# Expert slots by indirect DMA in place of dense experts, and a wfc bias taken into the matmul

## The reference, cut to what matters

```python
    x = x + jnp.tanh(g_xattn[0]) * _L0_xattn_ref(_layernorm(x), ctx_1024, ...)
    x = x + jnp.tanh(g_ffn[0]) * _L0_ffn_ref(_layernorm(x), L0_ffn_Wr, L0_ffn_We)
# attention: q, k with rms_norm for each head, softmax, then
        return x @ Wfc + fc_b
# experts: C = 97
        top_vals, top_idx = jax.lax.top_k(logits, K)
        w = jax.nn.softmax(top_vals, axis=-1)
        pos_all = jnp.cumsum(oh, axis=1) - oh
        keep = pos < C
        buf = jnp.zeros((Bb * Ee * C, Dd)).at[dst].add(x_rep, mode='drop')
        expert_out = jnp.einsum('becd,edf->becf', expert_in, We)
        gathered = jnp.take(expert_out, dst, axis=0, mode='fill', fill_value=0.0)
        out = jnp.einsum('btk,btkd->btd', w, gathered)
```

## Time and profile before

| what | value |
|---|---|
| time, median of 3 runs | 1391.57 us (1390.58 to 1393.33) |
| span of the profiled execution | 1388.5 us |
| TensorE busy | 1364.6 us, 98% |
| VectorE busy | 1046.5 us, 75% |
| ScalarE busy | 913.9 us, 66% |
| GpSimd busy | 775.2 us, 56% |
| granted TensorE clock, mean | 0.996 of full speed |
| data moved by DMA | 53.72 MB, mean 39 GB/s |

### The profile page before, as it was taken

The page is one execution under the profiler, slowest core; times in us unless marked ns, Lnnn a source line. Parts: engine busy times, 40 slices in busy tenths (PEclk is TensorE's granted clock), DMA queues, the critical chain, the costliest instruction groups (busy, mean ns, idle before and its releaser), DMA issues. The chain is left out here.

```text
span 1388.5 us, 26883 instructions
## 1 busy us (share of the span) xinstructions
PE 1364.6 (98%) x8116; PEld 1137.0 (82%) x8116; DVE 1046.5 (75%) x3057; ACT 913.9 (66%) x2600; POOL 775.2 (56%) x947
## 2 busy tenths in 40 slices
PE   7899999999999999999999999999999999999998
PEld 6688888888888888888888888888888888888876
DVE  6877877777877777877778777778777788777763
ACT  6776666775666766667766667666677666676652
POOL 4355555656555656555555566565555555555644
PEclk9999999999999999999999999999999999999999
DMA  5001101011111011110111010111110110101000
GB/s 164 30 18 46 45 28 45 18 45 45 37 37 45 18 46 45 32 42 25 38 45 45 29 45 18 45 45 36 38 39 24 45 45 31 43 18 46 25 16 23
DMA packets 70289, 53.72 MB, mean 39 GB/s; under 512 B 45888, under 2 KB 53504, under 8 KB 70144
## 3 DMA queue, kind: packets, MB, share of 16 engines
q1 hardware_dynamic: 70144, 52.00, 12.1%
HBM read 25.11 MB, written 16.78 MB: 30 GB/s over the span
## 5 line engine op out<-in xcount | busy, mean ns | idle before, releaser
L332 PE MATMUL bkM<-we,x2T 128*128 128x512 f32 x3072 | 791.7, 400 | 0.8 <-DVE acc_v L1067 0.7
L332 PEld LDWEIGHTS bkM<-we,x2T 128*128 128x128 f32 x3072 | 553.6, 188 | 127.6 <-ACT a_out L684 8.4
L684 ACT ACTIVATE a_out<-bkM,gate 128x256 f32<-128x256 f32 x512 | 217.0, 482 | 161.1 <-PE bkM L332 159.9
L1067 DVE SCALAR_TENSOR_TENSOR acc_v<-bkM,gate,acc_v 128x256 f32<-128x256 f32 x384 | 184.8, 481 | 106.2 <-PE bkM L332 91.3
L498 POOL TENSOR_TENSOR a_sum<-a_sum,a_out 128x256 f32<-128x256 f32 x256 | 188.9, 738 | 56.8 <-ACT a_out L684 20.5
L485 POOL TENSOR_TENSOR probs<-probs,p_inv 128x308 f32<-128x308 f32 x128 | 89.8, 702 | 211.6 <-DVE p_inv L960 211.6
L453 POOL TENSOR_TENSOR rstd<-ve,minus_half 128x4 f32<-128x4 f32 x64 | 65.2, 1019 | 145.6 <-DVE ve L872 145.4
L453 POOL TENSOR_TENSOR q_r<-q_ve,minus_half 128x8 f32<-128x8 f32 x64 | 105.0, 1642 | 48.6 <-DVE q_ve L945 48.6
L590 ACT ACTIVATE xn<-x_sb,shift,rstd 128x256 f32<-128x256 f32 x128 | 66.5, 590 | 92.4 <-DVE shift L881 92.4
L453 POOL TENSOR_TENSOR k_r<-k_ve,minus_half 77x8 f32<-77x8 f32 x32 | 52.4, 1637 | 126.9 <-DVE k_ve L921 126.9
L503 POOL TENSOR_TENSOR y<-a_sum,acc_v 128x256 f32<-128x256 f32 x128 | 94.4, 738 | 17.3 <-issue 0.4
(11 more groups left out here) (178 smaller groups left out, 2714.7 us busy)
## 6 DMA issues: line engine op xcount, KB each, us to landing
x_sb<-in_x SPq DMA_DIRECT2D x32, 512.0 KB, 3.7
out<-y SPq DMA_DIRECT2D x64, 256.0 KB, 2.0
ctx_sb<-in_ctx SPq DMA_DIRECT2D x32, 154.0 KB
vf<-v_nat SPq DMA_DIRECT2D x64, 77.0 KB
stage<-in_L_ffn_We SPq DMA_DIRECT2D x2, 1024.0 KB, 7.1
vf<-v_nat SPq DMA_DIRECT2D x32, 52.0 KB
vf<-v_nat SPq DMA_DIRECT2D x32, 51.0 KB
vf<-v_nat SPq DMA_DIRECT2D x32, 26.0 KB
```

The lines of the kernel that those rows point to most:

```text
L332: mm = nc.tensor.matmul(out, l, r, start=(i == 0), stop=(i == len(terms) - 1))
L684: ins = nc.scalar.activation(a_out[:, t % 2, (e // 4) * 2 + i], bkM[1][:, i * D:(i + 1) * D], ACT.Copy, scale=gate[:, m.parity, t, e:e + 1])
L1067: nc.vector.scalar_tensor_tensor(out=acc_v[:, t], in0=bkM[0][:, i * D:(i + 1) * D], scalar=gate[:, m.parity, t, e:e + 1], in1=src, op0=ALU ...
```

## The change

**Experts.** Instead of all experts for all tokens, the tokens' rows are sorted into expert slots through DRAM. `place` computes for each token and each of its two choices a row number. GpSimd scatters the rows of xn2 with indirect DMAs of 128 rows each, 4 for each batch, 8 for each pair. SyncE loads the slots back as 112 partitions of 8 rows (`load_rows`). Then eight units for each pair follow, of two experts of one batch: TensorE transposes 97 rows by 2 experts (4 transposes into the one bank bkM), ScalarE writes the hi part, VectorE the lo part, TensorE multiplies (12 matmuls of 256 columns into the one bank bkN), ScalarE copies out. SyncE stores the outcome (`store_rows`, two for each batch), GpSimd gathers with 8 indirect DMAs for each pair, and VectorE weights and adds both rows of each token (`combine`). Rows above the capacity of an expert stay zero in the outcome. The tables `T_AT` and `E_AT` say in which slot a unit is transposed and multiplied; units 6 and 7 and the product of unit 5 fall in the next round, where the pair is called c. The pipeline has one round more. x1 has three buffers, xn2 two.

**Bias.** fc starts each tile with two matmuls of a row of ones by the gated bias (hi, lo), and the residual reads the loaded x. GpSimd's four xb additions go.

Core of the diff:

```diff
+ROWS = 2 * LQ * (E // 2) * TOPK
+PAD = 112
+UNITS = BP * E // 2
...
+        slots_in = stage
+        slots_out = sb("slots_out", [P, 2, E // 2 * D])
+        slots_T = sb("slots_T", [P, 2, 2, KC * 2 * CAP], F32R)
+        fetched = sb("fetched", [P, TOPK, T, D])
...
+        in_d = [nc.dram_tensor(f"in_rows{b}", (ROWS, D), F32, kind="Internal").ap() for b in range(BP)]
+        out_d = [nc.dram_tensor(f"out_rows{b}", (ROWS, D), F32, kind="Internal").ap() for b in range(BP)]
...
-        front_banks_in_fill = [bkM[0], bkM[1]]
+        front_banks_in_fill = [bkM, bkN]
         kv_bank = [bkD, bkE]
...
+        T_AT = {7: (0, 0), 8: (0, 1), 9: (0, 2), 10: (0, 3), 11: (0, 4), 12: (0, 5), 2: (1, 6), 3: (1, 7)}
+        E_AT = {8: (0, 0), 9: (0, 1), 10: (0, 2), 11: (0, 3), 12: (0, 4), 1: (1, 5), 3: (1, 6), 4: (1, 7)}
+        def unit_at(table, k, c, m):
+            late, u = table.get(k, (0, None))
+            pair = (m, c)[late]
+            return (pair, u) if u is not None and pair else None
...
-            for n in range(PAIRS):
-                step(pair(n), pair(n + 1), pair(n + 2), pair(n + 3))
+            for n in range(PAIRS + 1):
...
+            def load_rows(m, b):
+                sp.wait_ge(stage_used, STAGE_USED)
+                sp.sem_inc(waits_alone, 1)
+                sp.wait_ge(scattered[b].sem, scattered[b].at(m))
+                sp.sem_inc(waits_alone, 1)
+                sp.wait_ge(unit_ps.sem, max(unit_ps.at(m, (b + 1) * UNITS_OF - UNITS), 0))
+                sp.sem_inc(waits_alone, 1)
+                sp.dma_start(slots_in[0:PAD, b], in_d[b][0:PAD * E].rearrange("(p j) d -> p (j d)", j=E)
+                             ).then_inc(rows_in[b].sem, 16)
+            def store_rows(m, b, i):
+                sp.wait_ge(expert_out.sem, expert_out.at(m, b * UNITS_OF + (i + 1) * UNITS_OF // 2))
+                sp.sem_inc(waits_alone, 1)
+                sp.wait_ge(gathered[b].sem, gathered[b].before(m))
+                sp.sem_inc(waits_alone, 1)
+                half = E // 2 * D
+                sp.dma_start(out_d[b][0:PAD * E].rearrange("(p j) d -> p (j d)", j=E)[:, i * half:(i + 1) * half],
+                             slots_out[0:PAD, i]).then_inc(rows_out[b][i].sem, 16)
...
+            def step(c, m, p, f, ahead):
+                if m:
+                    load_rows(m, 0)
+                if c:
+                    store(c, 0)
+                    store_rows(c, 1, 0)
+                if f:
+                    put_v(f)
+                if m:
+                    load_rows(m, 1)
+                if c:
+                    store_rows(c, 1, 1)
                 if ahead:
                     load(ahead)
-                if f:
-                    put_v(f)
-                store(m, 0)
-                store(m, 1)
+                if c:
+                    store(c, 1)
+                if m:
...
+            def scatter(m, b):
+                pool.wait_ge(cleared, CLEARS)
+                pool.sem_inc(waits_alone, 1)
+                pool.wait_ge(place_chain.sem, place_chain.at(m))
+                pool.sem_inc(waits_alone, 1)
+                pool.wait_ge(rows_in[b].sem, rows_in[b].before(m))
+                pool.sem_inc(waits_alone, 1)
+                for t in range(b * SUB, (b + 1) * SUB):
+                    for k in range(TOPK):
+                        nc.gpsimd.indirect_dma_start(
+                            out=in_d[b], out_offset=bass.IndirectOffsetOnAxis(ap=idx[:, m.parity, k, t:t + 1], axis=0),
+                            in_=xn2[:, m.parity, t], in_offset=None).then_inc(scattered[b].sem, 16)
+            def gather(m, b):
+                for i in range(2):
+                    pool.wait_ge(rows_out[b][i].sem, rows_out[b][i].at(m))
+                    pool.sem_inc(waits_alone, 1)
+                for t in range(b * SUB, (b + 1) * SUB):
+                    pool.wait_ge(y_done[t].sem, y_done[t].before(m))
+                    pool.sem_inc(waits_alone, 1)
+                    for k in range(TOPK):
+                        nc.gpsimd.indirect_dma_start(
+                            out=fetched[:, k, t], out_offset=None, in_=out_d[b],
+                            in_offset=bass.IndirectOffsetOnAxis(ap=idx[:, m.parity, k, t:t + 1], axis=0)
+                        ).then_inc(gathered[b].sem, 16)
+            def round_of(c, m, p, f):
                 if f:
                     ln1(f)
                 if m:
-                    finish_tile(m, 0)
+                    scatter(m, 0)
                 if p:
                     ln2(p)
+                if m:
+                    scatter(m, 1)
                 if f:
                     k_rsqrt(f)
-                if m:
-                    finish_tile(m, 1)
-                if f:
-                    make_xb(f, 0)
...
-                    make_xb(f, 3)
-                    make_xb(f, 2)
-                    normalise(f, 0)
-                    normalise(f, 1)
...
+            def unit_hi_part(m, u):
+                act.wait_ge(unit_ps.sem, unit_ps.at(m, u + 1))
+                act.wait_ge(expert_ps.sem, max(expert_ps.at(m, u - 1), 0))
+                copy(slots_T[:, u % 2, 0], bkM[:, 0:KC * 2 * CAP]).then_inc(unit_hi.sem, 1)
+            def expert_part(m, u):
+                b, i = divmod(u, UNITS_OF)
+                act.wait_ge(expert_ps.sem, expert_ps.at(m, u + 1))
+                h = i // 2
+                act.wait_ge(rows_out[1 - b][h].sem, rows_out[1 - b][h].at(m) if b else rows_out[1 - b][h].before(m))
+                act.wait_ge(cleared, CLEARS)
+                copy(slots_out[0:CAP, h, i % 2 * 2 * D:(i % 2 + 1) * 2 * D], bkN[0:CAP]).then_inc(expert_out.sem, 1)
...
+            def slot(k, c, m, p, f, xn_made=False):
+                next_unit(k, c, m)
                 if k == 0 and p:
                     o_part(p, 1)
...
                     if f:
                         exps(f, 0)
-                    chunk(k, m, p)
+                    unit_out(k, c, m)
                     if f:
...
                     if f:
                         o_part(f, 0)
+                if k != 9:
+                    unit_out(k, c, m)
 
...
             def residual(p, i):
                 dve.wait_ge(fc_ps.sem, fc_ps.at(p, i + 1))
-                dve.wait_ge(xb_done.sem, xb_done.at(p))
+                dve.wait_ge(x_in[p.parity], 16 * p.half + 16)
                 if i == 0:
                     dve.wait_ge(xn2_done.sem, xn2_done.before(p))
-                dve.wait_ge(v_added.sem, v_added.before(p, 2))
+                for t in range(T):
+                    dve.wait_ge(y_done[t].sem, y_done[t].before(p, X1_BUFS))
                 ts = slice(2 * i, 2 * i + 2)
-                nc.vector.tensor_tensor(x1[:, p.parity, ts], fc_bank[i][:].rearrange("p (t d) -> p t d", d=D),
-                                        xb[:, ts], ALU.add).then_inc(x1_done.sem, 1)
+                nc.vector.tensor_tensor(x1[:, p.n % X1_BUFS, ts], fc_bank[i][:].rearrange("p (t d) -> p t d", d=D),
+                                        x_sb[:, p.parity, ts], ALU.add).then_inc(x1_done.sem, 1)
                 dve.wait_ge(x1_done.sem, x1_done.at(p, i + 1))
...
+            def place(p):
                 dve.wait_ge(pos_done.sem, pos_done.at(p))
-                dve.wait_ge(v_added.sem, v_added.before(p, 2))
-                dve.wait_ge(a_ready.sem, a_ready.before(p, 2))
+                dve.wait_ge(top2.sem, top2.at(p))
+                nc.vector.tensor_tensor(placed[:], mask[:].rearrange("p k t e -> p k (t e)"),
+                                        pos_ps.unsqueeze(1).to_broadcast([P, TOPK, T * E]), ALU.mult
+                                        ).then_inc(place_chain.sem, 1)
+                dve.wait_ge(place_chain.sem, place_chain.at(p, 1))
+                nc.vector.tensor_reduce(row[:], placed[:].rearrange("p k (t e) -> p (k t) e", e=E), AX.X, ALU.add
+                                        ).then_inc(place_chain.sem, 1)
                 for b in range(BP):
-                    nc.vector.scalar_tensor_tensor(
-                        out=gate[:, p.parity, b * SUB:(b + 1) * SUB],
-                        in0=pos_ps.rearrange("p (s b e) -> p b s e", s=SUB, b=BP)[:, b], scalar=float(CAP),
-                        in1=g_all[:, b * SUB:(b + 1) * SUB], op0=ALU.is_lt, op1=ALU.mult
-                    ).then_inc(gate_chain.sem, 1)
...
+            def unit_lo_part(m, u):
+                dve.wait_ge(unit_hi.sem, unit_hi.at(m, u + 1))
+                lo(slots_T[:, u % 2, 1], bkM[:, 0:KC * 2 * CAP], slots_T[:, u % 2, 0]).then_inc(unit_lo.sem, 1)
...
+            def combine(c, b):
+                w = w_top[:, c.parity]
+                dve.wait_ge(gathered[b].sem, gathered[b].at(c))
+                dve.wait_ge(y_out[b].sem, y_out[b].before(c))
+                for t in range(b * SUB, (b + 1) * SUB):
+                    nc.vector.scalar_tensor_tensor(out=y[:, t], in0=fetched[:, 0, t], scalar=w[:, 0, t:t + 1],
```

(58 more changed lines are left out.)

309 lines of the change are left out of this document (126 added, 183 removed).

## The result

| | before | after |
|---|---|---|
| time, median | 1391.07 us (1389.38 to 1393.33) | 1679.91 us (1679.37 to 1687.64) |
| span of the profiled execution | 1388.5 us | 1677.9 us |
| granted TensorE clock, mean | 0.996 | 0.935 |
| data moved by DMA | 53.72 MB, 39 GB/s | 246.90 MB, 147 GB/s |

The changed kernel is slower by a ratio of 1.209 (95% interval 1.206 to 1.212). The forecast was 1495 us with a range of 1290 to 1590: the direction was right, the size was not, and the time lies outside the range.

What follows compares the result with a forecast made beforehand. TensorE's own stream sets today's 42.2 us round; after the change in-order waits make it 45.0. 1388.5 + 30 x 2.8 + 19 = 1491.5 of span, with 3.1 more 1495 us; range 1290 to 1590.

Steps and rivals of the forecast that it cites:

- the walk: One steady round followed in order from R, when TensorE is free after the last attend product; next R at 45.0.
- the ends: Fill unchanged in sum; after the last attend three rounds in series, 74 us instead of 55.5, +19.
- what bounds it: After the change, in-order waits between engines' streams; by work alone the round could close in 35 us.
- the clock: TensorE's clock counted at its full level, 1.00, despite idle pieces of 1 to 2 us.
- 8 bias matmuls of 256 columns at 1.41/12, 0.9: In fc on TensorE: the added bias matmuls cost 0.9 us a round.
- X: Time one indirect DMA of 128 rows holds GpSimd: taken as 1.1 us, with 0.87 and 1.64 kept.
- the middle: Exponentials: added hi parts, copies and waits put exps(3) at 36.6; with the combine's wait for gathers, 37.6.
- C: Rival: GpSimd becomes the bound; with X = 2 the round takes 50 us, the time 1645; chance 0.12.
- A: Rival: the round closes faster than the walk says, as streams' phases settle otherwise; 40.5 us, 1360; chance 0.23.
- B: Rival: TensorE's work alone decides; round of 37 us, 1255; chance 0.10.
- The load's landing: SyncE's load of 896 KB of rows takes 6.2 us, ahead of the store and gathers the combine waits for.
- Gap's 0.5 us: VectorE's gap priced at 0.2 us; 0.5 stays wherever normalise runs beside it, at most 1 us a round.

Runs made afterwards that it cites:

- combo: Changed kernel with 128-row ones and bias, unit 6 transposed ahead of fc, k_r ahead of the second scatters, rows' store ahead of load in SyncE's queue: 1537.20 us.
- bias_alone_rows: Kernel before with only the bias moved into fc, no xb additions, ones and bias operands of 128 rows: 1421.35 us.
- k_first: Changed kernel with GpSimd's k_r ahead of the second half's four scatters and a store of rows ahead of the load in SyncE's queue: 1640.07 us.
- combo_late_store: combo with VectorE's combine moved from slot 10 to the end of slot 12, and SyncE's output store put behind two stores of expert rows: 1492.42 us.
- units_only_xb: Changed kernel without scatters, gathers, row loads and stores, combining constant rows; unit 6 transposed ahead of fc, bias added on GpSimd: 1377.48 us.
- bias_alone: Kernel before with only the bias part of the change: one-row bias matmuls in fc, no xb additions, residual reads x: 1470.03 us.
- early6: Changed kernel with unit 6 transposed at step 1, ahead of the fc product instead of behind it: 1638.03 us.
- combo_store: combo with SyncE's output store put behind two stores of expert rows, the combine still in slot 10: 24 us slower than combo.

## Why the prediction was right in sign and wrong in size

Positions from R in the round at 865.59, against the walk:

| step | walk | measured |
|---|---|---|
| fc ends | 5.45 | 7.04 |
| unit 6's low part ends | 7.0 | 8.66 |
| shift | 8.7 | 10.3 |
| x_transpose | 10.9 | 12.6 |
| q | 14.6 | 17.0 |
| k_transpose | 18.7 | 21.8 |
| exps(0) | 27.5 | 31.3 |
| exps(3) | 37.6 | 41.6 |
| next R | 45.0 | 49.4 |

Two steps of the prediction failed: the round's sum, 45.0 where the settled rounds take 50.0, in the terms below, and the ends, +19 where they took +59. The waits themselves were right.

- **Right: what bounds it.** The waits that the walk named are in the trace at their places: VectorE idle 4.36 us ahead of unit 6's low part, x_transpose waiting for xn1, k_transpose for kn and kn for k_r, the second row maximum (0.67 us), unit 4's transposes behind unit 3's low part (1.49), the combine for its gathers (0.89). Three edits on them (unit 6's place; k_r's together with SyncE's order; the combine's on top of combo) gave back 1.3, 1.0 and 1.1 us a round by the traces.
- **The missing 5.0 us, in the walk's order.** Up to x_transpose 1.7, of which the bias is 1.6; from there to k_transpose 1.4; to exps(3) 0.9; to the next R 0.4. That is the round of the table, the only one wholly at the full clock. The other 0.6 go with the clock, as below.
- **Mis-sized: the bias.** The step "8 bias matmuls of 256 columns at 1.41/12, 0.9" was priced by full-height matmuls. The columns are right (bias_alone_rows: 0.98 a round), but the one-row operand costs 1.5 more. As it stands at the very front of the chain, the first four rows of the table are late by it and by little else. It is 49 us in the kernel before and 45 in the changed one, a quarter of what the forecast missed.
- **Mis-sized: X.** Taken as 1.1, measured 1.27. The four scatters between layernorm 2's power and k_r take 5.1 us instead of 4.4. That, a power of 1.2 us, and its start at 13.0 instead of 10.7 (1.6 of this is the bias) put k_transpose at 21.8. That the price matters from about there was right: k_r waited for scatters (k_ve ready at 883.27, k_r started at 884.91), and in k_first k_transpose is 1.4 us earlier; the round became 1.0 shorter.
- **Mis-sized: the middle.** From k_transpose to the fourth exps 19.8 us pass instead of 18.9; the combine's wait (1.1 us a round by combo against combo_late_store) was in the walk. What the walk did not say is that this wait takes back what is won ahead of it.
- **The clock.** The prediction counted it at its full level and said that no row showed otherwise. In the changed kernel 1 of the 28 settled rounds is wholly at that level, 49.4 us; 18 have a mean of 0.97 and take 49.5; 9 are at 0.93 or 0.90 and take 51.0. That is 0.6 us a round in the mean, some 17 us. That the lower level lengthens a round, and is not only its companion, is shown in combo_late_store alone.
- **The rivals.** C (GpSimd as the bound at X = 2, 1645) is the nearest number but not the cause: GpSimd is busy for 49% of the span, X is 1.27, and changing the order alone removes the delay. A's round of 40.5 isn't there: even units_only_xb, with no rows moved at all, has 41.8. B fails on order as the walk said; TensorE's own work in the round came to 38.3 us of busy time where 34.4 of work were summed. The bias is 1.6 of the difference (2.5 instead of 0.9); the rest is not divided, and busy time also counts a last matmul's way to PSUM at each piece of idle time.
- **The load's landing.** Estimated at 6.2 us by the rows' slope, measured 5.6, with the store behind it at 4.2. The fit of the Trainium skill ("DMA: Bandwidth & Descriptors", Anatomy of one DMA), 4.1 us, is further off; the page gives it for DMAs that GpSimd issues, and this load is SyncE's.
- **Wrong: the ends.** The step "router, place, scatters, load, units, store, gathers: 74, that is +19" gave +59. It put the last pair's place at 29 us and let the scatters follow it. VectorE's half of the router stands behind `combine`, which waits 7.29 us for gathered rows, and the place ends at 1605.09, 41.3 us after the last R at 1563.80:

```profile
1598.49 0.88 DVE L1127 SCALAR_TENSOR_TENSOR y<-fetched,w_top,x 128x256 f32<-128x256 f32 x2 [7.29 <-DMA fetched<-out_rows,idx]
...
1604.92 0.17 DVE L1108 SCALAR_TENSOR_TENSOR idx<-row,first 128x8 uint32<-128x8 f32 x1
```

  Then the scatters follow the gathers of the pair ahead in GpSimd's queue, 6.3 us more:

```profile
1606.38 0.95 POOL L563 DMA_INDIRECT fetched<-out_rows,idx  x1 [9.71 <-DMA out_rows<-slots_out]
...
1611.41 1.00 POOL L550 DMA_INDIRECT in_rows<-xn,idx  x1 [0.30 <-issue]
```

  so the first stands 47.6 us after that R, where the walk's router ended at 28. From there to the end 66.5 us pass instead of some 46. TensorE stands still for 6 to 7 us, for loaded rows or for a low part that is queued behind a combine, and then has the lower of its two clock levels (12 matmuls in 2.86 us instead of 1.64); over these last 114 us its granted clock is 0.70 in the mean:

```profile
1643.21 0.91 PE L1300 MATMUL bkM<-ident,stage 97*128 97x97 f32 x4 [6.03 <-DVE slots_T L919]
1643.82 2.86 PE L356 MATMUL bkN<-we,slots_T 128*97 128x256 f32 x12
```

- **The range.** It left room for X = 1.64 alone and none for several terms off the same way. 4.8 us a round over 30 rounds, of which about 1.5 is the bias, and 40 us of ends make the 185 missed.
- **Gap's 0.5 us.** It went, and what gap waits for can be read off the traces: a normalise on GpSimd. Before and after (VectorE's gap, then GpSimd's normalise, one round each):

```profile
732.21 0.69 DVE L1004 TENSOR_TENSOR gap<-top 128x4 f32<-128x4 f32 x1
```

```profile
732.18 0.70 POOL L485 TENSOR_TENSOR probs<-probs,p_inv 128x308 f32<-128x308 f32 x1 [1.85 <-DVE p_inv L960]
```

```profile
906.24 0.22 DVE L1063 TENSOR_TENSOR gap<-top 128x4 f32<-128x4 f32 x1
```

```profile
905.75 0.70 POOL L537 TENSOR_TENSOR probs<-probs,p_inv 128x308 f32<-128x308 f32 x1 [3.55 <-DVE p_inv L1019]
```

  Wherever the two overlap, in 31 of 32 gaps before and in 30 of 32 after, gap ends 0.02 us behind the normalise; without one beside it gap takes 0.16 us. In all but the first of them gap began 0.03 us behind the normalise's start before, and took its whole length; now it begins 0.5 us behind, and 0.2 us are left of it. That agrees with the rule of the Trainium skill ("SBUF — State Buffer", Who interferes with whom): gap has two SBUF inputs, and the normalise reads SBUF. Its 0.5 us went because the phase of the two shifted, and not by anything in the price of 0.2: that part of the sum came out by luck.

## What to carry to other kernels

In a pipeline of in-order streams, price a change by walking one round, and sum each term at the form it really has: a matmul operand of one row, or a DMA that GpSimd issues, has no near neighbour in the old trace and deserves a bound of its own at every place where it stands on the chain. When a step moves on one engine, move with it everything that waits for it in other queues, or the store behind it will hold up work that has nothing to do with it. Where two chains meet, as attention and the gathered rows do in the combine, shortening one gives back only what the other leaves. And walk the last rounds by the loop's own order, not by what the data would allow.

## What the hardware showed that was not expected

- A pair of 256-column float32r matmuls with one contraction row took 0.42 us, with 128 rows 0.24 us, and the six full ones behind it 0.91 instead of 0.71. The weight loads of the pair, in bias_alone and in bias_alone_rows, took the same:

```profile
340.33 0.29 PEld L1243 LDWEIGHTS bkA<-bias_r,ones_r 1*128 1x128 f32 x2
```

```profile
330.82 0.31 PEld L1243 LDWEIGHTS bkA<-bias_r,ones_r 128*128 128x128 f32 x2
```

  That agrees with the Trainium skill ("TensorE: Matmul & The Clock Gate", LDWEIGHTS), by which a load goes by its columns and not by its rows. So the loads are not longer. The single records of bias_alone show that they are later: where one row and 128 rows follow each other, in either direction, the next weight load begins 0.20 us after the start of the matmul ahead of it and the one behind that 0.11 us after, where the others begin together with the matmul ahead. From one matmul's start to the next it is then twice 0.20 to 0.23 us, where it is 0.11 to 0.12 in the rest of the six and everywhere in bias_alone_rows. Two such changes in a tile make the 0.38 us. So it is the change that is dear here; a long row of one-row matmuls was not run, and why the load comes late is open.
- Each indirect DMA of 128 rows held GpSimd for 0.97 us and 0.30 more to the next; scattered rows landed after 2.4 us in the changed kernel and 6.2 in early6, gathered ones after 2.8 in the changed kernel and 6.3 in combo_store (medians).
- What a stretch at the lower clock costs depends on where it falls. In the changed kernel's round from 816.12 (mean clock 0.97) the exponentials start at 32.6 instead of the 31.3 of the next round, but attend at 45.9 instead of 45.8, and the round is 49.5 against 49.4 us: the next round waits 0.89 us for gathered rows in its combine, and this one, later there, not at all. Over attend, in combo_late_store, such a stretch costs 0.8.
- The load of x, 512 KB, landed after 7.5 us instead of 3.7, at a mean traffic of 147 GB/s instead of 39. A single wait of 1.2 us is put down to it.
